# Reordering the passage from attention to the experts in a one-core block kernel

## What is computed

```python
x = x + attn(_layernorm(x))           # 16 heads of 16, rotary, softmax plus a linear-attention term, gated
# the experts, on xf = _layernorm(x):
logits = xf @ router_w.T              # (1024, 8)
top_v, top_i = jax.lax.top_k(logits, K)              # K = 2
probs = jax.nn.softmax(top_v)
g = jnp.einsum('th,efh->etf', xf, gate_w)            # E = 8 experts, F = 688, H = 256
u = jnp.einsum('th,efh->etf', xf, up_w)
y = jnp.einsum('etf,ehf->eth', jax.nn.silu(g) * u, down_w)
out = jnp.einsum('te,eth->th', combine, y)           # combine: probs at the two chosen experts
```

## Time and profile before

| | us |
|---|---|
| median of 3 runs | 442.66 (439.78 to 443.24) |
| the profiled execution | 444.38 |
| its span, first to last instruction | 442.5 |
| PE busy in it | 403.9 (91%) |
| DVE, ACT, POOL busy | 254.1, 206.5, 123.6 |

### The profile page before, as it was taken

How to read it: one execution, slowest core, us unless ns; L and a number is a source line. 1 busy time by engine, 2 the same in 40 slices (tenths; PEclk the granted TensorE clock), 3 DMA queues, 4 the chain that set the end, 5 groups by cost and what they waited for, 6 DMA issues and landing times.

```text
span 442.5 us, 6916 instructions
## 1 busy us (share of the span) xinstructions
PE 403.9 (91%) x2374; PEld 231.7 (52%) x2375; DVE 254.1 (57%) x511; ACT 206.5 (47%) x393; POOL 123.6 (28%) x122
## 2 busy tenths in 40 slices
PE   6897979999999999999997999889799999999891
PEld 2453744222222222422321234789689988997891
DVE  7499779878888887689797210656121331112130
ACT  4328736776767676566665796221111211121120
POOL 8016783140302012011035032018511112322312
PEclk9699769999999999999999899999799999999998
DMA  7126905547432608030032196416322121321332
GB/s 266 43 79 101 308 25 95 99 128 244 120 142 63 197 1 272 0 118 11 2 128 99 40 377 188 152 50 201 72 40 33 32 43 24 50 33 28 37 107 25
DMA packets 22876, 45.05 MB, mean 102 GB/s; under 512 B 4448, under 2 KB 15584, under 8 KB 22016
## 3 DMA queue, kind: packets, MB, share of 16 engines
q0 software_dynamic: 9216, 30.28, 24.0%
q1 hardware_dynamic: 13008, 13.74, 11.9%
q10 hardware_dynamic: 624, 0.66, 0.5%
HBM read 23.76 MB, written 15.59 MB: 89 GB/s over the span
## 4 chain that ended last, share of the span: by engine, by line
PE 74%; DVE 15%; issue 3%; DMA 2%; another core or an unknown queue 2%; ACT 2%; POOL 1%; DVEq 0%; POOLq 0%; ACTq 0%
PE psum L1360 71%; DVE mem L1071 8%; DMA mem<-weights 2%; ACT mem L891 1%; DVE mem L1136 1%; PE psum L1499 1%; PE psum L1630 1%; DVE mem L1249 1%; DMA mem<-x 1%; DVE mem L985 1%; POOL mem L586 0%; PE psum L1525 0%; DVE mem L1075 0%; PE psum L1412 0%
## 5 line engine op out<-in xcount | busy, mean ns | idle before, releaser
L1360 PE MATMUL psum<-mem 128*32 128x512 f32 (+15 forms) x2242 | 391.8, 409 | 24.6 <-DVE mem L1071 7.1
L1360 PEld LDWEIGHTS psum<-mem 128*128 128x128 f32 (+8 forms) x2242 | 217.1, 148 | 186.3 <-issue 81.2
L1071 DVE TENSOR_REDUCE mem<-psum 128x1 f32<-128x1024 f32 x128 | 152.1, 1219 | 32.3 <-PE psum L1360 29.9
L891 ACT ACTIVATE mem<-psum 128x512 f32<-128x512 f32 x256 | 137.6, 604 | 62.2 <-PE psum L1360 59.9
L1236 DVE COPY mem<-mem 128x3 f32<-128x3 f32 x18 | 3.3, 184 | 92.7 <-PE psum L1630 84.6
L908 ACT ACTIVATE mem<-psum 128x384 f32<-128x384 f32 (+3 forms) x32 | 15.0, 472 | 83.5 <-PE psum L1360 81.0
L722 POOL DMA_INDIRECT sum_d<-mem x17 | 26.6, 1562 | 80.0 <-ACT mem L916 60.3
L680 POOL DMA_DIRECT2D mem<-gate_up x21 | 15.3, 731 | 107.6 <-DMA mem<-mem 107.6
L916 ACT ACTIVATE mem<-psum,mem 128x256 f32<-128x256 f32 x18 | 8.5, 474 | 40.8 <-PE psum L1360 38.7
L1249 DVE TENSOR_TENSOR mem<-mem,psum 128x384 f32<-128x384 f32 (+3 forms) x32 | 15.5, 525 | 5.4 <-ACT mem L908 3.6
L698 POOL DMA_INDIRECT xg_d<-mem x16 | 15.7, 983 | 4.8 <-issue 4.8
(11 more groups left out here) (128 smaller groups left out, 199.0 us busy)
## 6 DMA issues: line engine op xcount, KB each, us to landing
xg_d<-mem POOLq DMA_DIRECT2D x8, 1036.0 KB, 9.6
mem<-gate_up POOLq DMA_DIRECT2D x8, 688.0 KB
mem<-gate_up POOLq DMA_DIRECT2D x8, 624.0 KB
mem<-down POOLq DMA_DIRECT2D x4, 1024.0 KB, 8.7
mem<-mem SPq DMA_DIRECT2D x54, 64.0 KB, 3.9
mem<-mem SPq DMA_DIRECT2D x18, 128.0 KB, 4.4
mem<-xg_d SPq DMA_DIRECT2D x16, 129.5 KB, 2.3
mem<-x SPq DMA_DIRECT2D x4, 256.0 KB, 3.2
```

Of the source, the lines that this page charges most:

```text
L891: nc.scalar.activation(prob[:, t % 8], psum[:, score_bank(n, t)], ACT.Exp, scale=HD ** -0.5).then_inc(exp_ready, 1)
L1071: V.tensor_reduce(mx[:, par, k:k + 1], banks(2 * (k % 2), 2), AX.X, ALU.max).then_inc(max_ready, 1)
L1360: return nc.tensor.matmul(*a, **k)
```

## The change

- **POOL**: `scatter(1)` stands in front of the DMAs of the last expert's gate and up weights.
- **ACT**: one SiLU of a single column is put right behind the last exponential, so that the table for SiLU is loaded there; `turned_copy(1, 1)` moves behind `tile_silu(0, 0)`.
- **DVE**: `hidden` is cut in two halves, which are placed singly in the passage: the first half of tile 0 stands ahead of the copy of the rows of tile 1, and the first half of tile 1 ahead of the norms.
- **PE, passage**: the transposes "combT" 1 stand in the middle of `gate_up(0, 1)`; those of "xn2T" in the middle of `gate_up(2, 0)`.
- **PE, tiles**: from g = 3 on, `turn_x` for the next tile stands between the two pieces of g, and waits only for the copy of the last rows that went through the same PSUM bank. For g = 4 (`LATE`) the rows are turned later, behind `down(3)`, and `down(4)` is done right behind them; g = 5 then has no `down`. For the last two g, `down(15)` and `down(16)` stand between the two pieces.
- A scratch word gets another name.

```diff
+        LATE = E - ENDS - 1
         def downs(g):
-            last = GATED.index(DIRECT - 2)
-            start = GATED[g - 1] if g - 1 != last else DIRECT
-            return range(start, GATED[g] if g != last else DIRECT)
+            own = (LATE, GATED.index(DIRECT - 2))
+            start = GATED[g - 1] if g - 1 not in own else GATED[g]
+            return range(start, GATED[g] if g not in own else GATED[g + 1])
...
             pool.wait_ge(lg_ps, 2)
+            scatter(1)
             for to, src in gate_up_pieces(gu[:, E - 1], gu_d[:, E - 1]):
                 pool.dma_start(to, src).then_inc(gu_in, 16)
-            scatter(1)
...
             attention(act, steps)
+            nc.scalar.activation(silu_1, half_c[:, 0:1], ACT.Silu)
             osb_copy(UNITS - 1, 1)
-            turned_copy(1, 1)
...
-            tile_silu(0)
-            tile_silu(1)
+            tile_silu(0, 0)
+            turned_copy(1, 1)
+            tile_silu(0, 1)
+            tile_silu(1, 0)
+            tile_silu(1, 1)
...
             for g in range(3, len(GATED)):
-                tile_silu(g)
+                tile_silu(g, 0)
+                if GATED[g] <= DIRECT:
+                    tile_silu(g, 1)
                 for t in downs(g):
                     tile_weigh(t)
+                if GATED[g] > DIRECT:
+                    tile_silu(g, 1)
...
             mix(UNITS - 1, NQ - 1, 1)
+            hidden_half(0, 0)
             xgT_copy(1)
             take_meta(1)
             for k in range(2):
                 add_x(1, k)
-                for n in (2 * k, 2 * k + 1):
-                    second_stats(1, n, last=n == 3)
-                if k == 0:
-                    hidden(0)
+            hidden_half(0, 1)
+            for n in range(4):
+                second_stats(1, n, last=n == 3)
             spreads(4, 8)
             xgT_copy(2)
+            hidden_half(1, 0)
             for n in range(4):
                 second_norm(1, 0, n)
+            hidden_half(1, 1)
             for n in range(4):
                 second_norm(1, 1, n)
-            hidden(1)
...
             for g in range(3, len(GATED)):
+                if g == LATE:
+                    hidden(g)
                 if g + 1 < len(GATED):
                     for n in rows_behind(g):
                         xgT_copy(n)
                         take_meta(n)
-                hidden(g)
+                if g != LATE:
+                    hidden(g)
...
             def turn_x(x):
                 pe.wait_ge(xg_in[x % 2], 16 * loads(x))
-                if x:
-                    pe.wait_ge(xgT_ready, x)
+                before = [n for n in range(x) if shared(ROWS_IN[n]) == shared(ROWS_IN[x])]
+                if before:
+                    pe.wait_ge(xgT_ready, before[-1] + 1)
...
-            gate_up(0, 1)
+            gate_up(0, 1, (0,))
             post(1, "combT", 1)
+            gate_up(0, 1, (1,))
             turn_x(1)
...
+            gate_up(2, 0, (0,))
             post(1, "xn2T", 2)
-            pe.wait_ge(xgT_ready, 3)
             post(1, "xn2T", 3)
-            gate_up(2, 0)
+            gate_up(2, 0, (1,))
...
             for g in range(3, len(GATED)):
-                for half in range(2):
-                    gate_up(g, half)
-                if g + 1 < len(GATED):
-                    for n in rows_behind(g):
+                gate_up(g, 0)
+                rows = rows_behind(g) if g + 1 < len(GATED) else ()
+                if g != LATE:
+                    for n in rows:
                         turn_x(n)
+                if GATED[g] <= DIRECT:
+                    gate_up(g, 1)
                 for t in downs(g):
+                    if t == GATED[LATE]:
+                        for n in rows:
+                            turn_x(n)
                     down(t)
+                if GATED[g] > DIRECT:
+                    gate_up(g, 1)
```

More of the change, by code:

```diff
@@ L219, in block_kernel @@
         row_i = keep(NMORE, dt=I32)
-        more_f = keep(1)
+        silu_1 = keep(1)
         more_i = keep(2, dt=I32)
@@ L917, in weigh, with tile_silu @@
                                             scale=weight_y[:, t:t + 1])
-            def tile_silu(g):
-                for half in range(2):
-                    act.wait_ge(gu_ps, 2 * g + half + 1)
-                    silu(half, wide(g)).then_inc(silu_ready, 1)
+            def tile_silu(g, half):
+                act.wait_ge(gu_ps, 2 * g + half + 1)
+                silu(half, wide(g)).then_inc(silu_ready, 1)
             def tile_weigh(t):
@@ L928, in tile_weigh @@
                 weigh(t).then_inc(y_ready, 1)
-            tile_silu(0)
-            tile_silu(1)
+            tile_silu(0, 0)
[3 more added lines that the diff above has]
+            tile_silu(1, 1)
             turned_copy(1, 2)
             turned_copy(1, 3)
-            tile_silu(2)
+            tile_silu(2, 0)
+            tile_silu(2, 1)
             tile_weigh(0)
@@ L1254, in times, with hidden_half @@
                 return ins
+            def hidden_half(g, half):
+                dve.wait_ge(silu_ready, 2 * g + half + 1)
+                if half == 0 and g >= NHID:
+                    dve.wait_ge(y_ps, last_use(g - NHID) + 1)
+                if half == 0 and g < NHID:
+                    V.memset(hidT(g)[FB[5]:FK[5], 5], 0.0)
+                times(half, g % NHID, wide(g)).then_inc(hid_ready, 1)
             def hidden(g):
                 for half in range(2):
-                    dve.wait_ge(silu_ready, 2 * g + half + 1)
-                    if half == 0 and g >= NHID:
-                        dve.wait_ge(y_ps, last_use(g - NHID) + 1)
-                    if half == 0 and g < NHID:
-                        V.memset(hidT(g)[FB[5]:FK[5], 5], 0.0)
-                    times(half, g % NHID, wide(g)).then_inc(hid_ready, 1)
+                    hidden_half(g, half)
             def take_meta(x):
```

## The result

The changed kernel takes 431.02 us (median of 4 runs, 428.42 to 432.46) beside 442.69 us of the kernel before (4 runs, 439.78 to 443.24). The ratio is 0.973, with an interval of 0.9692 to 0.9769: 11.7 us less, where 12.1 had been forecast. The profiled execution took 431.24 us, 13.1 less than that of before.

A forecast was written before the change was run, and what follows sets the result against it. PE was taken as the bound, busy 91% of the span with 74% of the chain. Passage 2.9, scatter and clock 5.9, tiles 3.3, end 0 sum to 12.1 us: 442.66 becomes 430.6 us, range 427.8 to 436.6.

The forecast's parts named there:

- Passage: Between attention and the tiles: PE's waits of 0.46, 1.63 and 1.14 us go but for 0.35, saving 2.9 us.
- Scatter: POOL's second scatter starts near 298 us: 0.35 to 0.65 us earlier by going before the weights, 2.9 by the passage.
- Turn between the pieces: At g = 3: an earlier turn removes PE's 2.96 us wait ahead of g = 4 and 2.95 of slow clock, 5.9 us.
- The lag of the signal: PE's turned rows reach DVE late during the second scatter: 4.25 us before, then between 1.64 and 4.25.
- The clock's 2.95 us: Tile g = 4 at 1.2 GHz after PE's wait took 8.08 us instead of 5.13; this extra was to go.
- the hold: During a scatter DVE or ACT takes PE's finished work late, "remote" named as releaser; forecast: it delays signals in the second half.
- the lag follows the scatter: Rival, ahead of g = 4: signals stay held some 13 us after the first indirect DMA; 436.4 us, chance 0.20.
- the row loads meet the weights: Rival: loads of row tiles 5 and 6 meet the last weights, costing 0.5 to 2 us; 432 us, chance 0.07.
- Tiles: At g = 4, 8 and 13: waits of 0.79, 0.79 and 1.71 us for late-turned rows go, 3.3 us.
- the slower rival: In 11 tiles the turn between pieces becomes a wait of 1.71 us each; 449.4 us, chance 0.03.
- End: Last tiles: 1.45 us new idle ahead of `down(17)`, offset by POOL's earlier additions; 0 us, bounds -0.7 and +0.5.

The follow-up runs named there:

- tile part alone: The kernel before with only the tile loops of the change; 434.08 us, ratio 0.9807.
- passage alone: The kernel before with only the passage changes (table load, halves of the first two tiles, transposes in the middle of pieces); 439.63 us, ratio 0.9952.
- swap undone: The changed kernel with the last weights issued in front of the scatter again; 431.41 us, ratio 0.9777.
- the tile part undone: The changed kernel with the tile loops of before, its passage and order on POOL kept; 437.27 us, ratio 0.9895.
- the late turn: The changed kernel with row tile 4 turned behind both pieces of g = 3; 434.65 us, 0.983 with the hold, and 427.0 us, 0.9848 without.
- second set: Group of follow-up runs whose traces show no hold; the kernel before had a median of 434.12 us there.
- the changed kernel again: The changed kernel run once more, nothing altered, in a set with the hold; 430.2 us, ratio 0.9741 to the kernel before.
- the end undone: The changed kernel with `down(15)` and `down(16)` behind both pieces of their tiles again; 427.8 us, ratio 0.9874.

## Why the prediction was right

**Passage: 2.9 forecast, 3.7 measured,** outside its bounds (2.0 to 3.2). All three waits went but for 0.15 us, where 0.35 had been left. That gives 3.1; as for the other 0.6, PE's timeline sums to less without the breaks (18.2 us in place of 18.8 for the same 160 records): a record's modelled end overlaps the next where PE runs on, so that each break hid some 0.2 us beside its idle time. That last reading is argued from the rows, not tested. The table load was priced rightly by its row: the SiLU behind it begins 1.30 us after the load (273.67 to 274.97).

**Scatter: the instant right, a step on the way wrong.** It starts at 297.56 ("about 298"), its last DMA is issued 3.7 us earlier (310.24 to 306.58), POOL's first addition 1.4 us earlier (311.51 to 310.10). But the swap was to bring the scatter forward by 0.35 to 0.65 us by itself, and it doesn't. The first DMA starts 2.17 us behind PE's turn of tile 3 (295.39), where it was 2.00 (301.26 against 299.26). It is 2.16 to 2.18 us in all seven profiles with the scatter in front of the weights, and 1.99 to 2.01 in the five with it behind them. The slots are ready at 296.57 + 0.17, and 0.82 us pass from there to the first DMA; with the weights in between it had been 0.65. The forecast instant came out because the passage gave 3.9 us at this place and not 2.9: two errors that offset each other.

**Turn between the pieces: right in what it does here, with less room than was thought.** The lag of the signal fell between the two bounds, 2.2 us, and PE never waited. Three terms deserve a second look. DVE's copy and first multiply were put at 1.2 us; by the rows it is 1.8 (DVE takes the rows at 314.23, and PE goes on at 316.06). So with the upper bound of the lag, rows at 309.1, PE would have waited some 0.9 us, not "a few tenths", and with the tile part alone it did wait 1.57 us and the clock fell. The clock's 2.95 us is the value of one profiled execution; in four other kernels with the wait, the slow stretch cost 1.5 to 1.7 us. With such a value the sum would have been about 10.8 us, and the closeness of 12.1 to the measured 11.7 owes something to luck. And the gain is there only where the hold is: without it the change is worth about 6.6 us, not 12. The wait of the earlier trace rows was taken for a fixed part of the kernel, and it isn't one.

**Rival "the lag follows the scatter": its mechanism was right, its price not paid.** In all eight profiles with the hold and the second scatter, the last signal held (ACT's second piece or DVE's rows) comes at a fixed distance behind the scatter's first DMA: 12.9 to 13.0 us where the weights stand in front of it (before, passage alone, tile part alone, swap undone), 11.5 us where they stand behind it (the changed kernel twice, the tile part undone, the late turn). So with the swap the hold ends 1.4 us earlier by the scatter and, as the scatter starts 0.17 us later, 1.2 us earlier by PE's list: as much as the wait of a kernel that still has one (3.44 to 2.21). Whether it is the weights in front that lengthen it is not shown. The swap also moves POOL's first addition, a ninth indirect DMA, from right behind the scatter to 2.56 us behind it, and no run separates the two.

The turn did not leave the held stretch. Sent 8.5 to 8.7 us into the scatter its signal lags by 3.0 to 4.25 us (four profiles). Sent 6.3 to 6.5 us into it, the lag is 2.2 in both profiles of the changed kernel, but 3.4 with the swap undone and 4.85 with the tile part alone. The place of the turn doesn't set the lag by itself. What it gives in any case is cover: when the turn is done PE still has the second piece of g = 3 and `down(2)` ahead of g = 4, some 5 us. That covered the 2.2 us and the chain behind them with about 1 us to spare (first multiply done at 307.22 + 0.56, g = 4 begun near 308.8), and did not cover the 4.85. Why the lag differs at the same place is open.

**Rival "the row loads meet the weights": came beside the forecast,** at its lower end: 0.45 us in the profile after, 0.6 and 0.9 in two profiles of the second set, none in two others of kernels with the swap (the changed kernel again, and the end undone), none with the swap undone. The additions show the crowding too: POOL's second one waited 5.34 us for the first where it was 2.49 (315.61), while 315 GB/s were moved. "DMA: Bandwidth & Descriptors" of the Trainium skill, section "Issuing engines are not separate DMA queues", says that DMAs of all issuing engines run on the same 16 DMA engines and interleave. The trace agrees: with POOL's weights on the way, SP's loads of 129.5 KB of rows took 5.2 us (median of two), where 2.3 us is the median of the kernel before.

**Tiles: 3.3 right.** The waits of 0.79, 0.79 and 1.71 are gone and no turn became a wait, so the slower rival is out.

**End: even in this profile, a small loss by the others.** PE ends 12.0 us earlier and the last addition starts 13.0 us earlier. The order of additions gave back most of the 1.39 us of new idle time: -1.39 + 1.02 = -0.4, inside -0.7 to +0.5. But what it gives back isn't fixed. In the seven profiles with the new end the last addition starts 1.5 to 3.0 us behind PE's last record, and in the seven with the old one 2.6 to 2.9, so nothing to 1.4 us come back. The step that failed in part is that the last addition no longer has to wait for the one before: it still does, and starts 1.27 us behind ACT's last result (421.38 + 0.47 to 423.12) where 0.77 had been put. The 0.8 us between the two traces named at "the end undone" is the best figure for the loss.

Sum by the rows: 3.7 + 5.9 + 3.3 - 0.45 - 0.4 = 12.05 us, beside 13.1 between the two profiled executions and 11.7 between the medians. Of the 13.1 us only 0.17 lie ahead of the passage. The other 0.9 have no row of their own; waits that are gone in the tiles, each with the 0.2 us of the passage's, would make about that (an estimate).

## What to carry to other kernels

Where a transpose or a load of the next tile stands ahead of a short piece of work and its copy is waited for right behind, put it one piece earlier: here 20 records of cover took away waits of 0.8 to 2.2 us and, together with the passage, one of 3 us; through the clock the longer ones had cost up to as much again. A wait whose releaser is "remote" should be priced with and without it, since it may be absent in another set of runs; the part of a gain that stands in plain waits (here 6.6 of 12 us) is the safe part. Before pacing or delaying a scatter, ask who reads the rows back: 7.4 us more for the writer were 6.18 us of standing for PE.

## What was not expected of the hardware

- While POOL has eight indirect DMAs of 128 rows under way, signals from PE reach DVE and ACT up to 4.85 us late from the scatter's middle on. The same signal, sent 6.3 to 6.5 us into the scatter, was 2.2, 2.2, 3.4 and 4.85 us late in four profiles. In the second scatter this ends 12.9 to 13.0 us behind the first DMA where 1.41 MB of weights have just been issued and an addition follows at once, and 11.5 us where the weights come between scatter and addition, four profiles each. It is present in two sets of runs (kernel before at 442.6 and 442.9 us) and absent in two (434.1 and 434.2). Removing the scatter removes it (0.42 us at that place). What in the scatter does it, and what makes a set show it, is open.
- The slow clock behind a wait has no fixed price: 2.95 us in the kernel before behind 2.96 us of waiting, 1.5 to 1.7 us in four other profiles behind waits of 1.6 to 3.4 us in all, nothing behind 0.66 us in two pieces (the swap undone).
- The kernel before is 2% faster in the sets without the hold, 8.6 us, more than the 5.9 us at tile 4 account for; 1.6 us of waiting and some slow clock (0.68 granted in 243 to 245) stand at the first scatter, and without the second scatter the two sets still differ by 2.4 us (435.69 and 433.29). No profile of the kernel before was kept in a set without the hold, so the rest is open.
